# Gated delta rule kernel: decay sums by a running sum on VectorE, level 0 of the inversion by a block transpose

## The reference, cut to what matters

```python
g = -jnp.exp(A_log) * jax.nn.softplus(a + dt_bias)     # log of the decay, per token and head
beta = jax.nn.sigmoid(b)
def step(S, xs):
    qt, kt, vt, gt, bt = xs
    S = S * jnp.exp(gt)[..., None, None]
    kv = jnp.einsum('bhk,bhkv->bhv', kt, S)
    delta = (vt - kv) * bt[..., None]
    S = S + jnp.einsum('bhk,bhv->bhkv', kt, delta)
    o = jnp.einsum('bhk,bhkv->bhv', qt * scale, S)
    return (S, o)
...
x = x + s * g
```

## Time and profile before

| | |
|---|---|
| median of three runs | 4563.17 us (4563.04 to 4564.75) |
| profiled execution | 4564.4 us, its span 4562.6 us |
| busy in the span: PE, DVE, ACT, POOL | 98%, 53%, 50%, 31% |
| mean granted PE clock | 0.996 |

### The profile page before, as it was taken

One profiled execution on the slowest core, in us unless ns is written; L12 is line 12 of the kernel. 1 busy time (PEld: TensorE's weight loads), 2 busy tenths in 40 slices (PEclk: granted clock), 3 DMA queues, 4 the chain that ended last, 5 costly groups with the idle time before them and its releaser, 6 DMA issues. The chain is left out here.

```text
span 4562.6 us, 79189 instructions
## 1 busy us (share of the span) xinstructions
PE 4488.8 (98%) x29480; PEld 3044.9 (67%) x29480; DVE 2438.0 (53%) x5386; ACT 2281.1 (50%) x5849; POOL 1431.0 (31%) x1542
## 2 busy tenths in 40 slices
PE   8999999999899999999999999999999999999999
PEld 4444444444677777777777777777777777777776
DVE  4232222220566666666666666665666666666664
ACT  1111111110466666666666656665666666666665
POOL 1000000000233333333333333333444444444444
PEclk9999999999999999999999999999999999999999
DMA  4000000002000000000000010010010000010001
GB/s 137 30 27 25 26 29 11 30 18 75 27 8 11 11 16 14 11 11 11 11 11 11 13 45 32 11 44 29 26 33 25 25 25 25 25 34 25 25 20 40
DMA packets 89694, 120.84 MB, mean 26 GB/s; under 512 B 29665, under 2 KB 46561, under 8 KB 89313
## 3 DMA queue, kind: packets, MB, share of 16 engines
q1 hardware_dynamic: 71360, 93.57, 6.1%
q10 hardware_dynamic: 17952, 22.21, 1.5%
HBM read 80.34 MB, written 35.42 MB: 25 GB/s over the span
## 5 line engine op out<-in xcount | busy, mean ns | idle before, releaser
L939 PE MATMUL bank<-xtile,wt 128*128 128x259 f32 x4096 | 1106.9, 394 | 24.6 <-DVE vraw L969 19.7
L939 PEld LDWEIGHTS bank<-xtile,wt 128*128 128x128 f32 x4096 | 715.9, 191 | 149.9 <-issue 49.5
L1304 ACT ACTIVATE xyinv<-bank 128x512 f16<-128x512 f32 x768 | 454.3, 597 | 326.6 <-PE bank L1243 324.0
L943 PE MATMUL bank<-wt,xtile 128*128 128x512 f32 x1024 | 537.5, 616 | 0.0
L1524 PE MATMUL bank<-wot,xnt 128*128 128x512 f32 x1024 | 529.0, 612 | 0.8 <-ACT xnt L1517 0.8
L1280 DVE TENSOR_TENSOR wlev<-bank,mask 128x256 f16<-128x256 f32 x768 | 319.8, 418 | 313.9 <-PE bank L1243 312.0
L969 DVE SCALAR_TENSOR_TENSOR vraw<-bank,taps,vraw 128x256 f32<-128x256 f32 x768 | 368.3, 481 | 117.7 <-ACT vraw L962 102.5
L1220 POOL TENSOR_TENSOR kend<-ktok,gts 128x256 f32<-128x256 f32 x256 | 151.4, 612 | 617.2 <-issue 617.0
L1243 PEld LDWEIGHTS bank<-xyinv,lth 128*128 128x128 f16 x3584 | 217.9, 97 | 186.3 <-issue 100.6
L1131 POOL TENSOR_TENSOR gm<-con,gts 128x512 f32<-128x512 f32 x128 | 133.2, 1041 | 640.3 <-PE bank L1160 472.6
L401 PE MATMUL bank<-h2t,wt 128*128 128x512 f32 x704 | 325.3, 606 | 0.8 <-DVE h2t L376 0.8
(11 more groups left out here) (181 smaller groups left out, 8841.5 us busy)
## 6 DMA issues: line engine op xcount, KB each, us to landing
xtile<-xt_scratch ACTq DMA_DIRECT2D x30, 518.0 KB, 3.8
xn<-x SPq DMA_DIRECT2D x32, 256.0 KB, 5.4
xt_scratch<-xt SPq DMA_DIRECT2D x8, 1024.0 KB, 5.7
g_scratch<-sel SPq DMA_DIRECT2D x32, 256.0 KB, 2.0
part_scratch<-prow SPq DMA_DIRECT2D x32, 256.0 KB, 2.0
prow<-part_scratch SPq DMA_DIRECT2D x32, 256.0 KB, 2.6
sel<-g_scratch SPq DMA_DIRECT2D x32, 256.0 KB, 3.0
sel<-x SPq DMA_DIRECT2D x32, 256.0 KB, 3.6
```

The source lines that it names most:

```text
L939: j = pe.matmul(b_p[:, 0:WIN], wt[:, k, c:c + P], xtile[:, par, k, :], **st)
L943: j = pe.matmul(b_p[:], xtile[:, par, k, HALO + cc * P:HALO + (cc + 1) * P], w, **st)
L1304: act.activation(dst, b_inv[p][:].rearrange("p (a h b s) -> p a h b s", a=2, h=HEADS, s=z), ACT.Copy).then_inc(s[f"xy_sb{p}"], 1)
```

## The change

The decay sums are no longer made by POOL and PE. The feed-forward stage transposes the log decays (one more small PE step and one ACT copy for each of its 8 units) and stores them as rows in DRAM. In attention, one DMA for each unit, issued from ACT's queue, repeats a row of 512 values on all 128 partitions (two buffers, two units ahead). DVE then forms (sum + value) x mask along the row with one `tensor_tensor_scan`, writes it to `gam`, and ACT takes exp in place. Level 0 of the inversion is made from `xyinv[.,1]`, which is zero outside 2x2 blocks, by one DVE transpose of 32x32 blocks. The feed-forward stage's small gate buffers move into the memory of `xtile`. The mask constant grows from 9 to 12 matrices. The core of the diff:

```diff
+def load_row(q, r, row_d, n):
+    c, m = divmod(n, NB)
+    g, c = divmod(c, CHUNKS // GROUPS)
+    q.dma_start(r["grows"][:, n % 2], row_d[c, g, m * HEADS * P:(m + 1) * HEADS * P].partition_broadcast(P)).then_inc(r[f"gr_in{n % 2}"], 16)
...
+            pe.transpose(bank[0][0:w, 3 * w:3 * w + P], dec, ident).then_inc(s["gc_ps"], 1)
...
+            act.activation(grow[:, u % 2], bank[0][0:w, 3 * w:3 * w + P], ACT.Copy).then_inc(s["gc_exp"], 1)
...
+                    sp.dma_start(row_d[u * NJ:(u + 1) * NJ].rearrange("j g (h p) -> (j g h) p", p=P), grow[:, u % 2]).then_inc(s[f"gt_out{u % 2}"], 16)
...
-        def pool_decay(pool, n):
...
-            pool.tensor_tensor(gm[:], le.unsqueeze(1).broadcast_to([P, HEADS, P]),
-                               rate(tile, cc, G_DEC)[:, unit_heads(m)].unsqueeze(2).broadcast_to([P, HEADS, P]), ALU.mult).then_inc(s["gm_sb"], 1)
...
         def pe_scores(pe, n):
...
-                pe.wait_ge(s["gam_sb"], n)
+                pe.wait_ge(s["kq_sb"], n)
...
-        def pe_decay(pe, n):
-
-            pe.wait_ge(s["kq_sb"], n + 1)
-            pe.wait_ge(s["gm_sb"], n + 1)
-            pe.matmul(b_a[:], gt, gm[:].rearrange("p h c -> p (h c)"), start=True, stop=True).then_inc(s["gam_ps"], 1)
+        def dve_decay(dve, n):
+
+            dve.wait_ge(s[f"gr_in{n % 2}"], 16 * (n // 2 + 1))
+            if n:
+                dve.wait_ge(s["pt_sb"], n)
+                dve.wait_ge(s["lt_sb"], n)
+            dve.tensor_tensor_scan(gam[:].rearrange("p h c -> p (h c)"), grows[:, n % 2], mask[:, M_PAST:, :].rearrange("p h c -> p (h c)"), 0.0, ALU.add, ALU.mult).then_inc(s["sum_sb"], 1)
 
         def act_decay(act, n):
             c, m, tile, cc = where(n)
-            act.wait_ge(s["gam_ps"], n + 1)
+            act.wait_ge(s["sum_sb"], n + 1)
...
-                i = act.activation(gam[:, h], b_a[:, h * P:(h + 1) * P], ACT.Exp, bias=rate(tile, cc, G_LNB)[:, v:v + 1])
+                i = act.activation(gam[:, h], gam[:, h], ACT.Exp, bias=rate(tile, cc, G_LNB)[:, v:v + 1])
             i.then_inc(s["gam_sb"], 1)
+            if n + 2 < UNITS:
+                act.wait_ge(s[f"gr_in{n % 2}"], 16 * (n // 2 + 1))
+                load_row(act, r, row_d, n + 2)
...
         def pe_level(pe, n, lv):
...
-                each_head(pe, b_inv[p], lambda h: lth[:, p, h], lambda h: ident16, f"w_ps{p}")
-                return
...
         def dve_level(dve, n, lv):
...
-                dve.tensor_tensor(xyinv[:, p, 0], quad(b_inv[p]), every(M_L0), ALU.mult).then_inc(s[f"w_sb{p}"], 1)
+                dve.wait_ge(s[f"y1_sb{p}"], u + 1)
+                dve.transpose(xyinv[:, p, 0].rearrange("p h c -> p (h c)"), xyinv[:, p, 1].rearrange("p h c -> p (h c)")).then_inc(s[f"w_sb{p}"], 1)
                 return
```

## The result

The changed kernel takes 4421.0 us, the median of 4 runs (4418.7 to 4424.0), beside 4563.1 us (4561.8 to 4564.8) for the kernel before on the same chip: a ratio of 0.9689, 95% interval 0.9672 to 0.9706, or 142 us less. The forecast was 4429 us in a range of 4403 to 4470.

What follows compares the result with a forecast made beforehand. The prediction took PE's own work in attention as the bound: the profiled 4564.4 us less 115 and 29, plus 1.5 and 8, gives 4430, or 4429 as median of runs; range 4403 to 4470.

Steps and rivals of the forecast that it cites:

- more is gained: Rival: removed PE groups also save type changes, old waits halve, no new waits come; 4407 us, chance 0.09.
- The decay step: On PE in attention: removing 128 fp32 matmuls of 512 columns saves 115 us, bounds 110 and 116.
- level 0: On PE in attention: removing 128 groups of four fp16 matmuls saves 29 us, bounds 28 and 36.
- The extra waits: PE in attention waiting for DVE steps pushed late by the new scan: 8 us, bounds 0 and 45.
- The feed-forward stage: Eight added fp32 transposes on PE ahead of attention, taken as 1.5 us more.
- The scan: New running sum on DVE for each unit in attention: 1.2 us, between bounds of 0.76 and 3.8.
- The transpose: New block transpose on DVE for level 0: 0.69 us, between 0.29 and 1.32.
- The issue: Row DMA issued from ACT for each unit: 0.53 us, hidden under exps of 1.1 us; uncovered 68 us in all.
- The exps: ACT's four exps per unit now read SBUF: 0.1 to 0.15 us more for each unit.
- Table loads: On ACT, exp table loads may rise from 95 by up to 33, at most 84 us of ACT; counted at zero.
- sign of being wrong: In the changed profile: table loads above 120 with ACT in PE's waits, among other signs.
- the slower rival: Scan near 3.8 us on DVE delays steps PE needs; decides above 1.12 us per unit; 4663 us, chance 0.07.

Runs made afterwards that it cites:

- e3: The changed kernel with one fp32 matmul of 512 columns added per unit ahead of the scores, its result overwritten: 4518.7 us, ratio 0.9898.
- e1: The changed kernel with level 0 of the inversion put back on PE, so the decay half alone: 4462.6 us, ratio 0.9775 to the kernel before.
- e2: The kernel before with level 0 made by the block transpose on DVE, the level 0 half alone: 4544.4 us, ratio 0.9955.
- r7: The changed kernel with each row load issued from ACT as two DMAs of 128 KB in place of one of 256 KB: 4420.9 us.
- s12: The changed kernel with the planner told a table load costs 1.6 us in place of 1.28, making 52 fewer in the whole program: 4421.6 us.
- s9: The changed kernel with each scan done three times in one step, the planner not told, so all lists keep their order: 4615.4 us, ratio 1.0109.
- e4: The changed kernel with each scan done three times in one step and the planner told 3.66 us: 4759.6 us, ratio 1.0429.
- r6: The changed kernel with each scan done twice in one step and the planner told 2.44 us: 4500.0 us, ratio 0.985.

## Why the prediction was right

**What bounds the kernel.** It rested on PE's own columns setting the time. They fell by 138 us, the forecast took 144 for them, and 142 came out; e3 shows the reverse, columns put back and time back. A us of PE's columns was worth 1.0 us in the whole change (142 / 138), 0.9 in e1 and e3 (102 / 110 and 98 / 110), and 0.7 in e2 (21 / 29). The rival *more is gained* had part of its way: 4421 lies between it, 4407, and the forecast.

**Terms of the sum.** The decay step was priced at 115 us and level 0 at 29; the halves' own columns give 110 and 29, and the runs 102 and 21. 110 is the decay step's lower bound: two records at the price of 0.429 us, with no change of type. The extra waits, taken as 8 us, are about nothing, and the rest of PE's time is 212 us where it was 215. The feed-forward stage was to be 1.5 us longer. These are the first projections of attention, before and then after:

```profile
1146.16 3.74 PE L939 MATMUL bank<-xtile,wt 128*128 128x259 f32 x16 [2.49 <-PEq L552]
```

```profile
1144.93 5.42 PE L958 MATMUL bank<-xtile,wt 128*128 128x259 f32 x16 [2.49 <-PEq L568]
```

They start 1.2 us earlier, but that is no measure of the 1.5: this start varies by 11 us between profiles with the same feed-forward stage. Added up for the profiled pair against the forecast: columns 6 us dearer (138 saved, not 144), the rest 11 us cheaper (-3, not +8), the first stage 2.7 us cheaper (-1.2, not +1.5). That is 8 us, by which the forecast was too high. Two terms were off in opposite directions, so it was in part luck that the sum came so close.

**The range.** Its lower end doesn't follow from its own words. The profiled 4564.4 less the upper bounds of the savings, 116 and 36, plus 1.5 and less 1.2 gives 4413, not 4403; 4421 lies inside either way.

**Prices on DVE.** The scan was taken as 1.2 us between bounds of 0.76 and 3.8, and is 1.215 at the median, 1.27 on average. The rows of before left a factor of five open; 1.2 is the figure of the changed list, and that it was right was judgement, not a result of the rows. The transpose was taken as 0.69, and is 0.71. DVE was to be at 71% and is at 69.6%. The Trainium skill's half throughput for the scan, on the page "DVE: opcode table, instruction layouts, handler registers and perf-mode slots", section "Datapath and trigger behaviour", agrees with this trace: the estimate of 1.07 us that was made from it lies 0.13 us under the shortest scan, 1.202 us. The scan's tail was expected up to 2.5 us, and ends at 1.603.

**Queues and ACT.** The issue hides (0.33 us under four exps of 1.3 us), twice over in r7. Rows land in 3.2 us, with a bound of 5.3. The exps take 390 ns on average where they took 372, 0.07 us for each unit and not 0.1 to 0.15. Table loads rose by 29, of the 33 allowed for. The prediction named as a sign of being wrong more than 120 of them with ACT in PE's waits, and both came: 124, and an eviction of ACT is PE's largest wait, 7.8 us where ACT's L1304 made 1.5 before. The sign was badly chosen: ACT is still at 68%, and s12 with 52 fewer is no faster. Counted at zero, they cost zero within the noise.

**Where the reasoning was weak.** The prediction said of a scan of 3.8 us that DVE would be at 81% and "on the mean it stays below PE in either case". That sentence gave no protection. s9 is that case, three scans of 1.2 us in the very order of after, and PE loses 194 / 128 = 1.5 us for each unit, more than the 1.12 from which the slower rival decides, and not far from the 1.9 that it assumed; it came out at 4615 us where it had 4663. With the planner's own order, e4, it is 4760. The mechanism of that rival is real; the forecast held because the scan is of the low price, not because DVE had room on the mean. r6 puts the loss for one more scan in a row, with an order of its own, at 79 us, or 0.6 us for each unit.

**What stays open.** The halves add up to 19 us less than the whole. Most of that is in the rest of PE's time (4 and 10 us more than before, where the whole has 3 less), and orders for unchanged work differ by up to 74 us; which decision of the planner makes it was not traced. Why it makes a worse order when it is told the true length of a long step (144 us between s9 and e4) is open too. The 194 us of s9 are mostly accounted for. The waits of PE that its trace names from 1193 us to the end make 166 us where after has 26. In attention PE was at the lower clock (half, 1.2 GHz) for 79 us where after was for 24, which costs at most half of the difference, 27 us. Together that is 167 us. e4 has 248 us of waits and 181 us at the lower clock: so of the 144 us between s9 and e4, 82 are waits and at most 51 the clock.

## What to carry to other kernels

When one engine is full, price a removed step from its start to the next start on that engine, and expect a little less than the sum. Work that is moved to an engine with room costs little only if its longest block is short against the slack of the small steps queued behind it: ask what stands behind one instruction and who waits for it, since 78% of load in short pieces cost 47 us here and the same scans in one block 194 to 339. An order from a planner is itself worth tens of us, so a difference of 1% between two of its orders is no evidence about the work in them.

## What the runs showed of the hardware

- A `tensor_tensor_scan` of 128x512 fp32 takes 1.20 us at the shortest and 1.215 at the median, 1.6 times the 0.76 us of an elementwise operation of that shape, and with an fp16 result about the same. These are the extra scans of s9:

```profile
L1176 DVE TENSOR_TENSOR_SCAN spent<-grows,mask x256: 1203/1224/1993, 1195.9 to 4539.0; 128x512 f16<-128x512 f32 x128
```

- The block transpose of 128x512 fp16 takes 699 to 712 ns in all 128 instances, while L1276, just ahead of it on the same tile, goes from 411 to 1225 ns. Here the operations with two sources in SBUF, L1276 and the scan (1.202 to 1.603 us), have long tails, and the transpose with one has none. In the Trainium skill, the page "SBUF — State Buffer" says in its section "Terms" that the loser of the shared port pair is fully blocked; the tail of L1276 agrees, and no run here took POOL's work away to test it.
- A DMA issued from ACT's queue runs ahead beside the activations: 0.33 to 0.45 us each, two behind each other under four exps, and r7 with twice the issues takes the same time (4420.9 and 4421.0 us).
- The kernels in which PE waits more are also granted the lower clock for longer. In attention after has 26 us of named waits and 24 us at half clock, r6 75 and 41, s9 166 and 79, e4 248 and 181.
